# A causal attention mask moved from GpSimd into a TensorE product

## The reference

```python
q, k = (l2norm(q), l2norm(k))
q, k = (q * srt, k * srt)                      # srt = 4
sim = jnp.einsum('bhid,bjd->bhij', q, k)
causal_mask = jnp.triu(jnp.ones((n, n), dtype=bool), 1)
sim = jnp.where(causal_mask, max_neg, sim)
attn = jax.nn.softmax(sim.astype(jnp.float32), axis=-1)
out = jnp.einsum('bhij,bjd->bhid', attn, v)
```

## Time and profile before

| | |
|---|---|
| time, 3 runs | 1076.33, 1081.10, 1081.51 us; median 1081.1 |
| profiled execution, its own time | 1082.78 us |
| its span, first to last instruction | 1081.0 us |
| mean granted TensorE clock | 0.932 |
| first step's values to last step's | 46.26 to 768.8 us |
| busy: PE / PEld / DVE / ACT / POOL | 902.4 / 672.9 / 619.5 / 545.8 / 236.9 us |

### The profile page before, as it was taken

How to read it: one execution, slowest core, us unless ns; L and a number is a source line. 1 busy time by engine, 2 the same in 40 slices (tenths; PEclk the granted TensorE clock), 3 DMA queues, 4 the chain that set the end, 5 groups by cost and what they waited for, 6 DMA issues and landing times.

```text
span 1081.0 us, 14277 instructions
## 1 busy us (share of the span) xinstructions
PE 902.4 (83%) x4446; PEld 672.9 (62%) x4446; DVE 619.5 (57%) x1383; ACT 545.8 (50%) x1032; POOL 236.9 (22%) x282
## 2 busy tenths in 40 slices
PE   3588998989898998969989898999871099999997
PEld 2466676667575765756757575766550077878775
DVE  3456777766666667657676666667576222222221
ACT  1356657566767664455666757676342122222221
POOL 3223322212112122222222222102102501111111
PEclk9688999999999999889999999999975599999999
DMA  8200000000000000000000000000344400000000
GB/s 274 53 1 1 1 2 1 1 1 1 1 1 1 1 1 1 1 1 1 1 1 1 1 1 1 1 1 1 117 139 164 144 11 20 27 21 29 20 25 4
DMA packets 19175, 29.02 MB, mean 27 GB/s; under 512 B 2079, under 2 KB 15648, under 8 KB 19104
## 3 DMA queue, kind: packets, MB, share of 16 engines
q1 hardware_dynamic: 17008, 22.73, 6.9%
q0 software_dynamic: 1680, 4.21, 1.1%
q10 hardware_dynamic: 416, 1.18, 0.3%
HBM read 21.41 MB, written 7.10 MB: 26 GB/s over the span
## 4 chain that ended last, share of the span: by engine, by line
PE 40%; DVE 6%; issue 3%; POOL 3%; ACT 3%; DMA 1%; DVEq 0%; ACTq 0%; POOLq 0%
PE W L1299 7%; PE S L1276 5%; PE O L1276 5%; PE O L1116 2%; PE W L1187 2%; PE S L1097 2%; PE S L1098 2%; PE O L1113 2%; PE O L1114 2%; PE W L1229 2%; POOL sorted_rows L596 2%; PE W L1209 1%; PE W L1155 1%; ACT hT L744 1%; DVE junk L969 1%
## 5 line engine op out<-in xcount | busy, mean ns | idle before, releaser
L849 DVE TENSOR_TENSOR pl<-pr,ph 128x512 fp32r<-128x512 f32 x288 | 199.2, 704 | 48.9 <-ACT pr L637 35.2
L635 ACT ACTIVATE ph<-S 128x512 fp32r<-128x512 f32 x224 | 135.0, 603 | 135.1 <-PE S L1098 133.0
L637 ACT ACTIVATE pr<-S 128x512 f32<-128x512 f32 x288 | 172.3, 600 | 27.9 <-PE S L1098 27.1
L1113 PE MATMUL O<-ph,vhi 128*65 128x512 f32 x288 | 140.8, 489 | 23.7 <-DVE ph L847 23.7
L1116 PE MATMUL O<-pl,vhi 128*65 128x512 f32 x288 | 117.8, 409 | 23.5 <-DVE pl L849 23.1
L1097 PE MATMUL S<-qT,kT 128*128 128x512 f32 x288 | 116.3, 404 | 0.0
L1114 PE MATMUL O<-ph,vlo 128*65 128x512 f32 x288 | 115.6, 401 | 0.0
L1098 PE MATMUL S<-qT,kT 128*128 128x512 f32 x288 | 115.4, 401 | 0.0
L543 POOL TENSOR_TENSOR rs<-ri,half 128x1 f32<-128x1 f32 x48 | 38.9, 811 | 233.5 <-DVE ri L782 233.4
L1116 PEld LDWEIGHTS O<-pl,vhi 128*65 128x65 f32 x288 | 39.9, 138 | 65.5 <-DVE pl L849 40.9
L752 ACT ACTIVATE gate<-S 128x512 f32<-128x512 f32 x38 | 20.7, 596 | 117.7 <-PE S L1276 117.7
(11 more groups left out here) (170 smaller groups left out, 1683.0 us busy)
## 6 DMA issues: line engine op xcount, KB each, us to landing
raw<-in_w_v SPq DMA_DIRECT2D x16, 512.0 KB, 6.3
wps<-in_w_proj SPq DMA_DIRECT2D x4, 1024.0 KB, 8.8
sorted_rows<-pad_row SPq DMA_DIRECT2D x19, 128.5 KB, 4.2
xs<-sorted_rows SPq DMA_DIRECT2D x19, 128.5 KB, 2.0
wqkv<-in_wqkv_t ACTq DMA_DIRECT2D x1, 1152.0 KB, 6.3
wout<-in_wout_t SPq DMA_DIRECT2D x1, 1024.0 KB, 10.0
xall<-in_x SPq DMA_DIRECT2D x1, 1024.0 KB, 10.7
xall<-in_x SPq DMA_DIRECT2D x1, 768.0 KB, 8.0
```

Of the source, the lines that this page charges most:

```text
L635: nc.scalar.activation(ph[:, k % RING, :], S[k % AHEAD][:], ACT.Exp, scale=SIM_SCALE)\
L637: nc.scalar.activation(pr[:, k % RING, :], S[k % AHEAD][:], ACT.Exp, scale=SIM_SCALE)\
L849: nc.vector.tensor_tensor(pl[:, k % RING, :], pr[:, k % RING, :], ph[:, k % RING, :].bitcast(F32), ALU.subtract).then_inc(pl_ready, 1)
L1113: nc.tensor.matmul(o, vhi[:, vs, 0:DH + 1], ph[:, k % RING, :], start=j == 0, stop=False)
```

## The change

The mask is put on before the exponential. A constant matrix `below` holds -64 where the key comes after the query and 0 elsewhere. In a step on the diagonal, TensorE first multiplies the identity with `below`, repeated for the 4 heads, into the bank of `S`, and the two score products add to it. The exponential has scale 16, so masked entries come out as exp(16 x (s - 64)), which is 0. With that all 288 steps have the form that only those off the diagonal had. GpSimd has no instruction in a step, VectorE has one, ScalarE two, and the semaphores `masked`, `ph_by_act` and `ph_by_dve` give way to `ph_ready`. At the start GpSimd makes one more constant (a memset and an affine_select), and VectorE makes fp32r copies of it and of the identity.

```diff
@@ -47,6 +47,7 @@
 ROW = DIM + 1
 EPS = 1e-5
 SIM_SCALE = 16.0
+MASKED = -64.0
 RING = 4
 KV = TPB + 2
 XS = 4
@@ -214,6 +215,9 @@
         xall = sb(keep, "xall", [P, TILES, ROW])
         ident = sb(keep, "ident", [P, P])
         half = sb(keep, "half", [P, HEADS + 2])
+        below = sb(keep, "below", [P, P])
+        below_r = sb(keep, "below_r", [P, P], F32R)
+        ident_r = sb(keep, "ident_r", [P, P], F32R)
         logits = sb(keep, "logits", [P, TILES, EXP])
         pos_i = sb(keep, "pos_i", [P, TILES], I32)
         expert_i = sb(keep, "expert_i", [P, SORTED + 1], I32)
@@ -358,9 +362,8 @@
         v_ready = sem("v_ready")
         s_ready = sem("s_ready")
         p_ready = sem("p_ready")
-        masked = sem("masked")
-        ph_by_act = sem("ph_by_act")
-        ph_by_dve = sem("ph_by_dve")
+        mask_ready = sem("mask_ready")
+        ph_ready = sem("ph_ready")
         pl_ready = sem("pl_ready")
         pv_done = sem("pv_done")
         ot_ready = sem("ot_ready")
@@ -437,15 +440,6 @@
 
             return steps[k][2] == steps[k][0] % TPB
 
-        diagonals = list(itertools.accumulate(int(on_diagonal(k)) for k in range(N_STEPS)))
-
-        def ph_wait(eng, k):
-
-            if on_diagonal(k):
-                eng.wait_ge(ph_by_dve, diagonals[k])
-            else:
-                eng.wait_ge(ph_by_act, k + 1 - diagonals[k])
-
         def freed_count(name, part, t):
 
             return freed[job_of[name, part, t]][1]
@@ -476,7 +470,7 @@
             load_x(2)
             sp.wait_ge(x_in[2], 16)
 
-            sp.wait_ge(consts, 10)
+            sp.wait_ge(consts, 12)
             for n in range(SORTED):
                 sp.dma_start(sorted_rows[n * P:(n + 1) * P, :], pad_row[:]).then_inc(pad_out, 16)
 
@@ -503,16 +497,20 @@
 
             nc.gpsimd.memset(ident[:], 0.0).then_inc(consts, 1)
             nc.gpsimd.memset(tri[:], 1.0).then_inc(consts, 1)
+            nc.gpsimd.memset(below[:], MASKED).then_inc(consts, 1)
             nc.gpsimd.memset(own[:], 1.0).then_inc(consts, 1)
             nc.gpsimd.memset(half[:], -0.5).then_inc(consts, 1)
             nc.gpsimd.memset(ones[:], 1.0).then_inc(consts, 1)
             nc.gpsimd.memset(pad_row[:], 0.0).then_inc(consts, 1)
-            pool.wait_ge(consts, 6)
+            pool.wait_ge(consts, 7)
             nc.gpsimd.affine_select(out=ident[:], in_=ident[:], compare_op=ALU.not_equal, fill=1.0, base=0,
                                     pattern=[[-1, P]], channel_multiplier=1).then_inc(consts, 1)
 
             nc.gpsimd.affine_select(out=tri[:], in_=tri[:], compare_op=ALU.is_gt, fill=0.0, base=0,
                                     pattern=[[1, P]], channel_multiplier=-1).then_inc(consts, 1)
+
+            nc.gpsimd.affine_select(out=below[:], in_=below[:], compare_op=ALU.is_gt, fill=0.0, base=0,
+                                    pattern=[[-1, P]], channel_multiplier=1).then_inc(consts, 1)
 
             nc.gpsimd.affine_select(out=own[:], in_=own[:], compare_op=ALU.is_ge, fill=0.0, base=0,
                                     pattern=[[-XD, 8], [0, CPAD]], channel_multiplier=1).then_inc(own_ok, 1)
@@ -525,7 +523,7 @@
             nc.gpsimd.iota(pad_row[:, DIM:ROW].bitcast(I32), pattern=[[0, 1]], base=TOKENS,
                            channel_multiplier=0).then_inc(consts, 1)
 
-            pool.wait_ge(consts, 10)
+            pool.wait_ge(consts, 12)
 
             def roots_of_x(n):
                 lo, hi = X_PARTS[n]
@@ -543,12 +541,6 @@
                 nc.gpsimd.tensor_tensor(rs2[:, n_root % LN, :], ri2[:, n_root % LN, :], half[:, 0:1], ALU.pow).then_inc(ln_root, 1)
 
             for k, stages in program("pool"):
-                if k is not None and steps[k][2] == steps[k][0] % TPB:
-
-                    pool.wait_ge(p_ready, k + 1)
-                    blk = pr[:, k % RING, :].rearrange("p (h q) -> p h q", h=HPG)
-                    nc.gpsimd.affine_select(out=blk, in_=blk, compare_op=ALU.is_ge, fill=0.0, base=0,
-                                            pattern=[[0, HPG], [1, P]], channel_multiplier=-1).then_inc(masked, 1)
                 for name, part, t, job in stages:
                     if name == "stats":
                         roots_of_x(part)
@@ -629,11 +621,9 @@
                     act.wait_ge(s_ready, k + 1)
                     if k >= RING:
                         act.wait_ge(pl_ready, k - RING + 1)
-                    if not on_diagonal(k):
-                        if k >= RING:
-                            act.wait_ge(pv_done, k - RING + 1)
-                        nc.scalar.activation(ph[:, k % RING, :], S[k % AHEAD][:], ACT.Exp, scale=SIM_SCALE)\
-                            .then_inc(ph_by_act, 1)
+                    if k >= RING:
+                        act.wait_ge(pv_done, k - RING + 1)
+                    nc.scalar.activation(ph[:, k % RING, :], S[k % AHEAD][:], ACT.Exp, scale=SIM_SCALE).then_inc(ph_ready, 1)
                     nc.scalar.activation(pr[:, k % RING, :], S[k % AHEAD][:], ACT.Exp, scale=SIM_SCALE)\
                         .then_inc(p_ready, 1)
 
@@ -827,25 +817,20 @@
             nc.vector.memset(vhi[:, :, DH:DH + 2].bitcast(F32), 1.0).then_inc(dconst, 1)
             nc.vector.memset(vlo[:, :, DH:DH + 2].bitcast(F32), 0.0).then_inc(dconst, 1)
 
+            dve.wait_ge(consts, 12)
+            nc.vector.tensor_copy(below_r[:], below[:]).then_inc(mask_ready, 1)
+            nc.vector.tensor_copy(ident_r[:], ident[:]).then_inc(mask_ready, 1)
+
             dve.wait_ge(w_in, 32)
             for c in range(CH):
                 nc.vector.tensor_scalar(wqkv[:, c, :], wqkv[:, c, :], g1c[:, c:c + 1], None, ALU.mult).then_inc(wq_scaled, 1)
 
-            diag = 0
             for k, stages in program("dve"):
                 if k is not None:
-                    t, _, j = steps[k]
-
-                    if j == t % TPB:
-                        diag += 1
-                        dve.wait_ge(masked, diag)
-                    else:
-                        dve.wait_ge(p_ready, k + 1)
+                    dve.wait_ge(p_ready, k + 1)
+                    dve.wait_ge(ph_ready, k + 1)
                     if k >= RING:
                         dve.wait_ge(pv_done, k - RING + 1)
-                    if on_diagonal(k):
-                        nc.vector.tensor_copy(ph[:, k % RING, :], pr[:, k % RING, :]).then_inc(ph_by_dve, 1)
-                    ph_wait(dve, k)
                     nc.vector.tensor_tensor(pl[:, k % RING, :], pr[:, k % RING, :], ph[:, k % RING, :].bitcast(F32),
                                             ALU.subtract).then_inc(pl_ready, 1)
                 for name, part, t, job in stages:
@@ -1083,7 +1068,7 @@
 
         @block.tensor
         def _(pe):
-            pe.wait_ge(consts, 10)
+            pe.wait_ge(consts, 12)
 
             def scores_of(k):
                 t, g, j = steps[k]
@@ -1094,7 +1079,12 @@
                     pe.wait_ge(act_freed, freed_count("q_turn", 4, t))
                 ks = (t - t % TPB + j) % KV
                 q = qT[t % 2][:, HPG * g:HPG * (g + 1), :].rearrange("p h q -> p (h q)")
-                nc.tensor.matmul(S[k % AHEAD][:], kT[:, ks, 0, :], q, start=True, stop=False)
+                if on_diagonal(k):
+                    if k == 0:
+                        pe.wait_ge(mask_ready, 2)
+                    nc.tensor.matmul(S[k % AHEAD][:], ident_r[:], below_r[:].unsqueeze(1).broadcast_to([P, HPG, P]),
+                                     start=True, stop=False)
+                nc.tensor.matmul(S[k % AHEAD][:], kT[:, ks, 0, :], q, start=not on_diagonal(k), stop=False)
                 nc.tensor.matmul(S[k % AHEAD][:], kT[:, ks, 1, :], q, start=False, stop=True).then_inc(s_ready, 1)
 
             def values_of(k):
@@ -1109,7 +1099,7 @@
                         pe.wait_ge(v_ready, 2 * (t + 1))
                 vs = (t - t % TPB + j) % KV
                 last = j == t % TPB
-                ph_wait(pe, k)
+                pe.wait_ge(ph_ready, k + 1)
                 nc.tensor.matmul(o, vhi[:, vs, 0:DH + 1], ph[:, k % RING, :], start=j == 0, stop=False)
                 nc.tensor.matmul(o, vlo[:, vs, 0:DH + 1], ph[:, k % RING, :], start=False, stop=False)
                 pe.wait_ge(pl_ready, k + 1)
```

## The result

| | before | after |
|---|---|---|
| median of all runs, us | 1081.12 (4 runs) | 1053.76 (4 runs, 1051.61 to 1057.11) |
| ratio to before | 1 | 0.9761, 95% interval 0.9731 to 0.9792 |
| span of the profiled execution, us | 1081.0 | 1052.9 |
| first step's values to last step's, us | 46.3 to 768.8 | 40.3 to 741.0 |

The change makes the kernel 27.4 us faster by the medians and 2.4% by the ratio. The forecast was 13 us and 1068, with a range that ended at 1053. The sign and the mechanism held, and the gain was twice as large as I had it. The time lies 6 us beyond rival A's 1060 and 0.8 us inside the end of the range, so that it lies in the range at all is in part luck.

A forecast was written before the change was run, and what follows sets the result against it. TensorE was taken to bound dense slots, with waits on top. Product +13.3, ScalarE +2, waits -24.0 and clock -4 sum to -12.7: 1070.1 us own time, 1068 against the median; likeliest band 1062 to 1075, range 1053 to 1083.

The forecast's parts named there:

- rival A: TensorE's low clock mostly goes with the waits, through 64 more products and fewer holes: another -8 us, 1060; chance 0.18.
- What bounds, and why TensorE waits: Dense slots are TensorE's, plus its waits; the long ones come from the mask queued behind `rn` on GpSimd.
- Waits removed: Mask and copy leave GpSimd and VectorE, so TensorE's waits shrink: -24.0 us, between -12 and -32.6.
- slots of tiles 2 and 10: Mask behind `rn` delays `on` and TensorE's transposes; 2 x 2.25 = 4.5 us gained, a new wait before L1116.
- only move to L1116: Three waits of 1.45 to 1.8 us before L1113, from VectorE's late copy, move to L1116; 1.3 us gained.
- The product, 0.23 us each: 64 added mask products on TensorE, less those falling in waits, plus some on low clock: +13.3 us.
- rival D: Repeated operand or weight switch makes each mask product 0.40 us, 25.6 in place of 13.3: 1081; chance 0.06.
- ScalarE, 2 us: 64 added exponentials `ph`, 31.4 us of ScalarE's time, of which 2 us taken as on the path.
- What was left out: VectorE's `pl` (mean 704 ns) shrinking where no GpSimd mask runs beside it; a few tenths a slot at most.
- Rival B: Waits only move to L1116 because VectorE is late; 12 us gained, clock stays: +1.3, 1082; chance 0.17.
- my sign of being wrong: Waits before L1116 growing over 10 us, or a slot like tile 14's lengthening beyond its four products' 0.9 us.
- The clock, -4: Three 3.4 us low-clock stretches behind removed TensorE waits go, 4.7 us if all; taken as -4, between 0 and -12.

The follow-up runs named there:

- Run 1: Kernel before, with only the inverse norms `rn` queued on GpSimd after the diagonal masks instead of in front: 1054.95 us, ratio 0.9763.
- Run 2: Changed kernel with the mask product issued twice in each of the 64 diagonal steps: 1066.04 us, ratio 0.9860.
- run 3: Changed kernel without the mask product, so the diagonal blocks are not masked at all: 1046.94 us, ratio 0.9679.
- Run 5: Changed kernel with one more exponential on ScalarE in each of the 64 diagonal steps, into an unread tile: 1056.84 us, ratio 0.9803.
- run 4: Kernel before, with zero-operand products filling four of TensorE's waits for `ph` (tiles 4, 5, 12, 13): 1080.03 us, ratio 0.9989.

## Why the prediction was right, and where its size was off

- *What bounds, and why TensorE waits.* Right. Run 1 shows it alone: only the order on GpSimd changed, and all the time came.
- *Waits removed, forecast 24.0 us, less 2 for ScalarE.* TensorE's idle time fell by 26.4, of which 3 would be products that fell into waits by the forecast: 23.4 otherwise. Right in sum, and the first step came as worked out (44.90 against 45.1). By place two errors nearly cancel, which is luck. In the slots of tiles 2 and 10 I took 4.5 us, since VectorE would wait for `rn` at `qn` and TensorE, in turn, 2 us before L1106. VectorE does (1.56 and 1.80 us), TensorE doesn't, and 9.0 us of waits for `on` went. Against that, 4.3 us of waits for `oT` came up. Of the three waits that "only move to L1116", two are waits of 1.28 and 1.29 us there now (165 and 536 us), and the one of 1.77 us is gone.
- *The product, 0.23 us each, +13.3 in all.* Run 2 gives 12.3 for another 64. Right as a price, which settles rival D. Taken out, it gives back only 6.8 (run 3).
- *ScalarE, 2 us.* Run 5 has 3 for the like amount by the medians and 6 within the steps. Of the 4.3 us more for `oT`, run 1 has 2.4 without any added work on ScalarE (13.4 us in all), which leaves about 2 for it.
- *What was left out.* The mean of `pl` is 698 ns where no mask runs on GpSimd and 704 before, 1.8 us of VectorE's time in all. Leaving it out was right.
- *Rival B.* The waits for `pl` grew by 2.5 us only; more than 10 was my sign of being wrong. The slot of tile 14 became 0.7 us longer (51.5 for 50.8), within its four products' 0.9.
- *The clock, -4, is the term that was mis-sized.* I counted three stretches whose wait went wholly and put the rest at the bound of -12. Of 44.4 us busy at 1.2 GHz 29.0 went, worth 13.3, with all eight stretches between 74 and 665 us gone but those of tiles 9 and 10, which shrank from 20.4 to 10.2 us. That is above even my bound. The forecast gave no reason for keeping those at 74.6, 98.5 and 173.6; that tiles 2 and 10 keep half of their wait stood against rival A, and it was no obstacle: a shorter wait brought no low stretch in most places. The 13.3 us are busy time. Where it can be counted in time saved, in run 4, half of it became waits again. Rival A had the clock at -12 and gave 1060, with 0.18; it deserved more, since many of the low stretches stood directly behind a wait that the change shortens.
- *Rival A's reason, more products,* is the lesser half: run 1 has none and got from 55.6 to 29.1 us, the changed kernel has 20.5.

What stays open: the worth of the whole lot of low stretches. It lies below the 13.3 us of busy time by as much as turned into waits, and differs by place: in tile 1 the stretch at 72 us costs the kernel without product 1.5 us (67.94 to 77.84 us between two third products, 67.57 to 76.01 in the changed kernel), in tiles 4, 12 and 13 one was worth half of that. Open is also why some waits have a low stretch behind them and others of the same length have none. In the kernel before the two of 1.93 us differ in this (280 us without, 661 us with).

## What to carry to other kernels

When an in-order engine with little work stands in a chain, look at what is queued in front of its instruction before moving the work elsewhere: here a reordering of one list gave the same 2.4% as a new product, a second exponential and a new constant. Removing a wait of TensorE can be worth more than its length, since the slow clock that followed it goes too (0.7 to 0.8 us each in run 4); price that for each wait that gets shorter, not only for those that vanish. Try the order of the other queues too: two stages placed later gave 7.6 us more, and one of them gave 8 us in the kernel before, where no queue had been freed.

## What the runs showed of the hardware

Products with an operand of zeros can keep the clock up: behind 12 of them (2.95 us) the granted clock was 1.00 where it had been 0.50. A product whose moving operand repeats 128 columns four times costs what a dense one does, 0.23 us from start to start (577.57 to 577.80, and 577.80 to 578.03 for the dense one behind it). In the kernel after, the waits before L1106 between 460 and 740 us (1.6 us at most) had no low stretch behind them, while that of 3.03 us at 449 us had one from 452.7 us on. It is not the length of that one wait alone: behind a wait of 0.89 us at 415.1 the clock was low from 415.2 to 418.6.
